# Attention, a triangle update and two norms: three engine queues in another order

## The chip, the core and the metric

The kernel runs on one core of a Trainium2 chip. The core has five engines that work through queues of their own, each strictly in program order: TensorE (PE, matrix products), VectorE (DVE), ScalarE (ACT, activations), GpSimd (POOL) and SyncE (SP, which issues the DMAs). They wait for each other on semaphores. A wait holds up all that is queued behind it on its engine. The metric is the time of one execution on the device in microseconds (us), and lower is better.

## The reference, cut to what matters

The input is 32 images of 16 x 16 pixels with 32 channels, in float32. Eight layers follow each other, each as `x = x + layer(norm(x))`. Only the parts that the change touches are shown.

```python
# layer 0: linear attention, 4 heads of 32
q = softmax(q, over channels) / sqrt(32);  k = softmax(k, over pixels);  v = v / 256
out = einsum(einsum(k, v), q) @ w_out + b_out;  out = norm(out) * ln_scale
# layer 1: spectral convolution over the 256 pixels, with filters made of phi, sigma, M_u, M_phi
# layer 2: "triangle"
a = sigmoid((x @ Wa1 + ba1) * (x @ Wa2 + ba2));  b = sigmoid((x @ Wb1 + bb1) * (x @ Wb2 + bb2))
g = sigmoid(x @ Wg + bg);  z = einsum('bikc,bkjc->bijc', a, b);  y = g * (norm(z) @ Wz + bz)
# layer 3: recurrent cell;  layer 4: scan over rows;  layer 5: mixture of experts
# layer 6: scan over rows;  layer 7: recurrent cell
norm(v) = (v - mean(v, over channels)) / sqrt(var(v, over channels) + eps)
```

## The kernel before, in words

**Layout.** The 128 partitions hold 4 groups of 32 channels (NQ = 4), and each group holds 8 images (G = 8) of 256 pixels. `xQ` is the running sum, of 2,048 columns, in four chunks (CH = 4) of 512 columns. In one cut a chunk is a pair of images, in another it is a quarter of the pixels of all images. `bank` is the accumulator memory of TensorE, eight banks of 512 columns.

**A norm** runs chunk by chunk through three engines. PE multiplies by a centring matrix (`ln_centre`, line 207), ACT squares (`ln_square`, L266), PE spreads the mean of the squares (`ln_spread`, L213), ACT takes Ln and Exp (`ln_rstd`, L272 and L277), and DVE multiplies (L259, L1303 and others). Two norms, number 2 (ahead of the spectral convolution) and number 7 (ahead of the second scan), read `xQ` in pairs of images and write it in quarters of the pixels. For quarters 0 and 1 they centre straight from `xQ`: `ln_centre_r` (L229) makes four products per quarter, each of 32 output rows and 512 columns that step by four elements through all images, so all of `xQ` must be there. For quarters 2 and 3, DVE first copies strips (`copy_strips`, L254), and PE centres the strips. DVE starts these copies when all of `xQ` is there. The order on PE is centre 0, centre 1, spread 0, centre 2, spread 1, centre 3, spread 2, spread 3.

**Attention** (PE L575 to L663, ACT L985 to L1045, DVE L1213 to L1265) works through 16 units u: K product, Q product, V product, transposition of exp(K), context product. Each engine has its loop over i, and lags the units:
- PE in step i: K(i), filters, Q(i), V(i), transpose(i-1) (L605), context(i-2) (L617), in every fourth step an output product, filters.
- ACT in step i: in steps 2 and 3 first two scalings of the spectral weights (L1028), then eviction of filters (`a_filters`, L1019), `a_k(i)` (Exp, L990), `a_kn(i-1)` (L1011), `a_v(i)` (L999), `a_q(i)` (Exp of Q, L1005); in step 0 then `filter_setup` (L961 to L967), which prepares the spectral weights; filters.
- DVE in step i: `v_k(i)` (maximum, L1216), `v_qw(i-1)` (L1234 to L1239, which needs `a_q(i-1)`), `v_q(i)` (L1223 to L1229), then the context scaling of unit i-2. In step 1 it also computes the fraction weights (L1201 to L1210), which ACT's scalings wait for.
- POOL: `q_normalise(u)` (L471), and behind units 1, 2 and 3 a sum of spectral weights (L487). The last of these sums releases the filters.

The 16 filters of the spectral convolution (`filters`, PE) stand two to a step, in steps 5 to 12. The second of a pair overwrites the accumulator of the first, so it waits for ACT's eviction, and the first of the next step waits likewise. After the sixteenth, SP issues 16 DMAs (L445) that spread the filters.

**Triangle.** Once the spectral convolution ends (L707), PE transposes the last quarter (16 small products), DVE adds it, and norm 3 of the last quarter follows (`normalise(3)`, L1303). Then PE makes the 16 `a` products, the 16 `b` products (128 x 128 each) and the gate. DVE adds a bias in halves (L1333) and multiplies (L1338) to get `a_in`, then `b_in`. ACT takes the sigmoid of `a` (L1069) and of `b` (L1073), and then copies three of eight masked blocks of `a` (`a_bd`, L1078, ACT_BD = 3), and DVE the other five (L1343). The 128 products of a with b (L745) wait for all of them.

**Experts.** Eight products (g = 0 to 7) end the layer; each pair fills one accumulator bank, and DVE adds it to `xQ` (L1539). Norm 7 comes next.

`keep_busy` (L532) issues products whose results nobody reads, between waits. A helper records `full` at L532 too, so many kinds of product show that line.

## Time and profile before

| | us |
|---|---|
| median of 3 executions (lowest, highest) | 474.16 (472.72, 477.4) |
| the profiled execution: its own time | 474.01 |
| its span in the trace | 471.9 |

Busy shares of the span: PE 90%, weight loads of PE 55%, DVE 52%, ACT 38%, POOL 7%. The profile has 2.11 us outside the span. Where stages lie in the trace, in us from the start of the span:

| stage | from | to |
|---|---|---|
| attention units, without filters | 17 | 47 |
| attention units with filters, and the last three | 47 | 112 |
| norm 1 and the sum; norm 2 | 112 | 136 |
| spectral convolution | 136 | 247 |
| triangle up to the products of a with b | 247 | 271 |
| rest of the triangle, recurrent cell, norm 5, scan, experts | 271 | 397 |
| norm 7 | 397 | 409 |
| second scan, recurrent cell, store | 409 | 472 |

A matmul in float32 shows as two records (x2), so that 8 products are x16.

### The profile page before, as it was taken

The numbers are of one execution on the slowest core, as the hardware profiler recorded it, in microseconds if no ns is written. First come the engines' busy times: TensorE is split into PE (matmuls) and PEld (weight loads), VectorE is DVE, ScalarE is ACT, GpSimd is POOL, SyncE is SP. The second block draws the span as 40 slices with busy tenths as digits, with TensorE's granted clock in tenths as the row PEclk, the third lists the DMA queues.
The fourth block names the chain that finished last, engine by engine and source line by source line (L and its number), as shares of the span: only waits on it lengthen the run. The fifth ranks groups of instructions, "written<-read, shape, count | busy, mean of one in ns | idle before, by whom it ended". The sixth has DMA issues, their size and how long they took to land.

```text
span 471.9 us, 7130 instructions
## 1 busy us (share of the span) xinstructions
PE 424.3 (90%) x2880; PEld 260.1 (55%) x2880; DVE 246.3 (52%) x486; ACT 181.3 (38%) x373; POOL 32.9 (7%) x39
## 2 busy tenths in 40 slices
PE   6967999999879999998999999897999899999990
PEld 2434656554255567653765555394475474475590
DVE  3499677786778050106103746646534628434735
ACT  1776777755530002001102643454504631414360
POOL 0037222222000000000000000000000000000000
PEclk8898999999999999999999999998999999999997
DMA  9940000079940000000002000000000000000003
GB/s 222 135 97 1 1 1 1 2 160 219 203 90 0 1 0 0 1 0 0 1 0 47 0 1 3 0 1 2 0 1 2 2 0 1 0 1 1 0 1 90
DMA packets 6479, 15.24 MB, mean 32 GB/s; under 512 B 2718, under 2 KB 5422, under 8 KB 5806
## 3 DMA queue, kind: packets, MB, share of 16 engines
q1 hardware_dynamic: 5870, 14.25, 14.9%
q8 instruction: 23, 0.38, 0.3%
q10 hardware_dynamic: 576, 0.52, 0.3%
q14 instruction: 10, 0.08, 0.1%
HBM read 5.86 MB, written 1.05 MB: 15 GB/s over the span
## 4 chain that ended last, share of the span: by engine, by line
PE 66%; DVE 17%; ACT 10%; issue 3%; DMA 1%; POOL 1%; POOLq 0%; SPq 0%; DVEq 0%; ACTq 0%
PE bank L673 20%; PE bank L532 17%; PE bank L213 6%; PE bank L861 5%; PE bank L207 4%; PE bank L806 4%; PE bank L817 3%; PE bank L229 2%; ACT lnv L272 2%; ACT rs L277 2%; DVE xn L259 1%; DVE xQ L1294 1%; DMA xR<-in_x 1%; PE bank L605 1%; ACT arena L1019 1%
## 5 line engine op out<-in xcount | busy, mean ns | idle before, releaser
L673 PE MATMUL bank<-xn,arena 128*128 128x512 f32 (+15 forms) x332 | 88.9, 427 | 2.4 <-DVE xn L259 2.4
L673 PEld LDWEIGHTS bank<-xn,arena 128*128 128x128 f32 x332 | 56.3, 190 | 36.0 <-issue 27.0
L266 ACT ACTIVATE sq<-bank 128x512 f32<-128x512 f32 x36 | 21.3, 591 | 118.0 <-PE bank L207 98.3
L532 PE MATMUL bank<-sb_consts 128*128 128x512 f32 (+1 forms) x116 | 52.9, 569 | 1.6 <-ACT arena L1153 1.6
L532 PE MATMUL bank<-xn,sb_w_attn 128*128 128x512 f32 x64 | 35.4, 644 | 4.8 <-ACT attn_scratch L990 3.7
L213 PE MATMUL bank<-sq,sb_consts 128*128 128x512 f32 x72 | 38.7, 623 | 0.7
L272 ACT ACTIVATE lnv<-bank 128x512 f32<-128x512 f32 x36 | 21.5, 597 | 35.4 <-PE bank L213 35.3
L1303 DVE TENSOR_TENSOR arena<-bank,rs 128x512 f32<-128x512 f32 x4 | 4.2, 1038 | 51.4 <-ACT rs L277 51.4
L532 PEld LDWEIGHTS bank<-sb_consts 128*128 128x128 f32 x116 | 20.5, 194 | 18.7 <-issue 16.5
L861 PEld LDWEIGHTS bank<-arena,sb_w_late 128*128 128x128 f32 x180 | 23.0, 191 | 11.1 <-DVE arena L1470 8.0
L861 PE MATMUL bank<-arena,sb_w_late 128*128 128x128 f32 x180 | 27.2, 287 | 1.7 <-DVE arena L1470 1.3
L806 PE MATMUL bank<-arena,sb_consts 128*128 128x128 f32 x144 | 27.7, 276 | 0.7 <-DVE arena L1420 0.7
L207 PE MATMUL bank<-xQ,sb_consts 128*128 128x512 f32 x40 | 23.0, 664 | 5.6 <-DVE xQ L1183 3.1
L817 PE MATMUL bank<-arena,sb_w_late 128*128 128x128 f32 x144 | 27.9, 276 | 0.0
L1294 DVE TENSOR_TENSOR xQ<-bank,xQ 32x128 f32<-32x128 f32 x48 | 18.3, 382 | 13.7 <-PE bank L673 13.1
L1107 ACT ACTIVATE arena<-bank 128x128 f32<-128x128 f32 x72 | 19.9, 277 | 14.3 <-PE bank L817 14.2
L213 PEld LDWEIGHTS bank<-sq,sb_consts 128*128 128x128 f32 x72 | 12.6, 193 | 21.8 <-issue 13.5
L471 POOL TENSOR_TENSOR attn_scratch<-attn_scratch 128x512 f32<-128x512 f32 x16 | 20.3, 1272 | 58.1 <-DVE attn_scratch L1239 57.9
L277 ACT ACTIVATE rs<-lnv 128x512 f32<-128x512 f32 x36 | 22.7, 629 | 1.1
L806 PEld LDWEIGHTS bank<-arena,sb_consts 128*128 128x128 f32 x144 | 21.7, 192 | 2.3 <-issue 2.3
L1470 DVE SCALAR_TENSOR_TENSOR arena<-bank,xn 128x128 f32<-128x128 f32 x30 | 8.7, 291 | 26.7 <-PE bank L861 25.9
L532 PEld LDWEIGHTS bank<-wvo,xn 128*128 128x128 f32 x128 | 17.7, 200 | 8.1 <-issue 8.1
(193 smaller groups left out, 623.5 us busy)
## 6 DMA issues: line engine op xcount, KB each, us to landing
arena<-arena SPq DMA_DIRECT2D x4, 1024.0 KB, 16.0
arena<-arena SPq DMA_DIRECT2D x4, 512.0 KB, 8.7
arena<-in_w_spec SPq DMA_DIRECT2D x2, 720.0 KB
sb_w_late<-in_w_late SPq DMA_DIRECT2D x1, 1100.5 KB, 22.8
xR<-in_x SPq DMA_DIRECT2D x4, 256.0 KB, 4.5
arena<-arena SPq DMA_DIRECT2D x4, 256.0 KB, 4.1
sb_w_attn<-in_w_attn SPq DMA_DIRECT2D x1, 641.0 KB, 7.4
arena<-in_w_spec SPq DMA_DIRECT2D x2, 256.0 KB
```

What stands on the lines that cost most here:

```text
L207: pe.matmul(bank[:, centre_bank(i), :], centre, src, start=True, stop=True).then_inc(S("ln_centred"), 1)
L213: pe.matmul(bank[:, var_bank(i), :], mean32, sq[:, i % 2, :], start=True, stop=True)\
L266: act.activation(sq[:, i % 2, :], bank[:, centre_bank(i), :], ACT.Square).then_inc(S("ln_squared"), 1)
L272: act.activation(lnv[:, i % 2, :], bank[:, var_bank(i), :], ACT.Ln, bias=LN_EPS[i // CH])\
L277: act.activation(rs[:, i % 2, :], lnv[:, i % 2, :], ACT.Exp, scale=-0.5).then_inc(S("ln_rstd"), 1)
L471: link(pool.tensor_tensor(qn[:, u % QN, :], qe[:, u % 2, :], qn[:, u % QN, :], ALU.mult))
L532: return mm(ps, lhsT, rhs, start=True, stop=True)
L673: return mm(bank[:, k, lo * B:hi * B], lhs, cols[:, at * B:(at + hi - lo) * B], start=start, stop=stop, **kw)
L806: mm(place(s, h), ident, z_[:, h, s % RES, :, :], start=True, stop=False)
L817: mm(place(s_, h), rvt[i], before(h, s_ % RES), start=False, stop=True)\
L861: last = mm(bank[:, 4 + h % 2, 0:P], band[i][:, w, :], carry[:, h - 1, w:w + 4, :], start=(w == 0), stop=(w == 2))
L1294: last = dve.tensor_tensor(xs, stu[C * r:C * r + C, :, G * q:G * q + G].rearrange("p t g -> p g t"), xs, ALU.add)
```

## The change

- Attention. PE: the step becomes K(i), transpose(i-1), Q(i), filters, V(i), context(i-2), ... . ACT: the step becomes (scalings in steps 2 and 3), `a_q(i-1)`, `a_kn(i-1)`, `a_k(i)`, filters, (in step 0 the rest of norm 0), `a_v(i)`, (in step 0 `filter_setup`), filters.
- Norms 2 and 7. PE centres quarters 0 and 1 in pieces: for each pair of images as soon as it is there, 8 products of 128 columns. In norm 2 this starts after the second pair. In norm 7 two of the four pieces stand within the experts' last products. The order behind is spread 0, centre 2, spread 1, centre 3, spread 2, spread 3.
- Triangle. The `a` products of the first three quarters stand in places of `keep_busy`, ahead of the last quarter's norm; DVE adds the first half of the bias ahead of `normalise(3)`. ACT copies two of its blocks of `a_bd` ahead of the sigmoid of `b`, and one behind. Products of `keep_busy` change from (3, 4) to (2, 2), and three single ones go.

```diff
-BUSY_ATTN, BUSY_TRI, BUSY_SCAN, BUSY_LOGITS = 4, (3, 4, 6, 1), 3, 2
+BUSY_ATTN, BUSY_TRI, BUSY_SCAN, BUSY_LOGITS = 4, (2, 2, 6, 1), 3, 2
-ACT_BD = 3
+ACT_BD, ACT_BD_FIRST = 3, 2
...
+        def centre_images(pe, k, j):
+            for q in range(STRIP_Q):
+                for r in range(NQ):
+                    last = pe.matmul(bank[C * r:C * r + C, q, 2 * TC * j:2 * TC * j + 2 * TC],
+                                     centre[:, C * q:C * q + C], xQ[:, 2 * j:2 * j + 2, r:T:NQ], start=True, stop=True)
+                if j == CH - 1:
+                    last.then_inc(S("ln_centred"), 1)
+
+        def ln_pe_images(pe, k):
+            def centre_strip(q):
+                pe.wait_ge(S("strips"), NQ_STRIPS * R_NORMS.index(k) + q - STRIP_Q + 1)
+                ln_centre(pe, CH * k + q, strips[:, q - STRIP_Q, :])
+            ln_spread(pe, CH * k)
+            centre_strip(2)
+            ln_spread(pe, CH * k + 1)
+            centre_strip(3)
+            ln_spread(pe, CH * k + 2)
+            ln_spread(pe, CH * k + 3)
...
# PE, attention
-                for m in filter_turn(u, 0):
-                    filters(m)
+            def attn_q_v(u):
+                j, q = divmod(u, NQ)
                 if u >= 1:
                     pe.wait_ge(S("q_shift"), u)
                 full(bank[:, 2, :], wq[:, q, :], flat(xn, j)).then_inc(S("q_ps"), 1)
+                for m in filter_turn(u, 0):
+                    filters(m)
...
                     attn_mid(i - 1)
+                if i < U:
+                    attn_q_v(i)
...
# PE, norm 2
-            ln_pe_r(pe, 2, xQ, lambda: pe.wait_ge(S("x_attn"), CH))
+            for j in range(CH):
+                pe.wait_ge(S("x_attn"), max(2, j + 1))
+                centre_images(pe, 2, j)
+            ln_pe_images(pe, 2)
...
# PE, triangle
-            keep_busy(BUSY_STU, 6)
+            def a_columns(ms):
+                for m in ms:
+                    pe.wait_ge(S("ln_applied"), 3 * CH + m // 4 + 1)
+                    last = full(bank[:, m // 4, (m % 4) * P:(m % 4 + 1) * P],
+                                xnH[:, m, :, :].rearrange("p g w -> p (g w)"), wa)
+                    if m % 8 == 7:
+                        last.then_inc(S("ab_ps"), 1)
+            pe.wait_ge(S("w_late_in"), 16)
+            a_columns(range(0, 4))
             pe.wait_ge(S("stu_rows"), 1)
...
-            keep_busy(BUSY_STU, 6)
+            a_columns(range(4, 8))
             pe.wait_ge(S("x_stu"), CH)
             ln_centre(pe, CH * LN_TRI + CH - 1, tokens(xQ, CH - 1))
-            keep_busy(1, 6)
+            a_columns(range(8, 12))
             ln_spread(pe, CH * LN_TRI + CH - 1)
             keep_busy(BUSY_TRI[0], 6)
             pe.wait_ge(S("ln_applied"), 4 * CH)
+            a_columns(range(12, 16))
...
# PE, norm 7, and within the experts' last products
-                    ln_pe_r(pe, k, xQ, lambda: pe.wait_ge(S("x_moe"), CH))
+                    for j in (2, 3):
+                        pe.wait_ge(S("x_moe"), j + 1)
+                        centre_images(pe, k, j)
+                    ln_pe_images(pe, k)
...
+                    if g in (5, 7):
+                        pe.wait_ge(S("x_moe"), g // 2 - 1)
+                        centre_images(pe, 7, g // 2 - 2)
...
# ACT, attention
+                if 0 <= i - 1 < U:
+                    a_q(i - 1)
+                    a_kn(i - 1)
+                if i < U:
+                    a_k(i)
                 for m in filter_turn(i, 0):
                     a_filters(m)
-                if i < U:
-                    a_k(i)
...
-                    a_q(i)
...
# ACT, triangle
+            act.wait_ge(S("a_s"), 1)
+            blocks_of_a(range(ACT_BD_FIRST))
             act.wait_ge(S("b_in"), 1)
...
+            blocks_of_a(range(ACT_BD_FIRST, ACT_BD)).then_inc(S("a_bd"), 1)
...
# DVE, triangle
+            link(add_ab_bias(0, 0))
             normalise(3)
...
+                    link(add_ab_bias(1, 0))
+                last = add_ab_bias(k, 1)
```

## Rows read from the trace of the kernel before

**Rows 1.** The page's chain of work that ended last, shares of the span by engine
```profile
PE 66%; DVE 17%; ACT 10%; issue 3%; DMA 1%; POOL 1%; POOLq 0%; SPq 0%; DVEq 0%; ACTq 0%
```

**Rows 2.** Timeline, PE in filter units: start, length, instruction, [idle before <- releaser]
```profile
51.40 1.12 PE L532 MATMUL bank<-xn,sb_w_attn 128*128 128x512 f32 x2
...
69.58 1.12 PE L532 MATMUL bank<-xn,sb_w_attn 128*128 128x512 f32 x2
...
71.12 0.82 PE L532 MATMUL bank<-sb_w_stu,arena 64*128 64x256 f32 x4 [0.42 <-ACT arena L1019]
...
75.39 1.13 PE L532 MATMUL bank<-xn,sb_w_attn 128*128 128x512 f32 x2
```

**Rows 3.** Timeline, ACT in the same unit
```profile
71.99 1.05 ACT L1019 ACTIVATE arena<-bank 128x512 f32<-128x512 f32 x1 [0.92 <-PE bank L532]
```

**Rows 4.** Timeline, ACT at the start of attention
```profile
25.05 0.84 ACT L967 ACTIVATE odd_sig<-sig 32x1 f32<-32x1 f32 x4
...
28.62 0.63 ACT L1005 ACTIVATE attn_scratch<-attn_scratch 128x512 f32<-128x512 f32 x1 [0.71 <-DVE attn_scratch L1229]
30.78 2.19 ACT L1028 ACTIVATE arena<-arena,fw 128x1024 f32<-128x1024 f32 x2 [1.52 <-DVE fw L1210]
```

**Rows 5.** Timeline, DVE at the start of attention, first of `v_qw(0)`, of `v_qw(1)`, and `v_k(4)`
```profile
24.79 0.70 DVE L1234 TRANSPOSE_TENSOR_REDUCE attn_scratch<-attn_scratch 128x16 f32<-128x512 f32 x1
...
31.20 0.70 DVE L1234 TRANSPOSE_TENSOR_REDUCE attn_scratch<-attn_scratch 128x16 f32<-128x512 f32 x1
...
40.66 0.69 DVE L1216 TENSOR_REDUCE attn_scratch<-bank 128x2 f32<-128x512 f32 x1 [0.67 <-PE bank L532]
```

**Rows 6.** Timeline, POOL and PE up to the first filter
```profile
43.15 1.27 POOL L471 TENSOR_TENSOR attn_scratch<-attn_scratch 128x512 f32<-128x512 f32 x1 [1.60 <-DVE attn_scratch L1239]
...
47.13 0.82 PE L532 MATMUL bank<-sb_w_stu,arena 64*128 64x256 f32 x4 [2.88 <-POOLq L489]
```

**Rows 7.** Timeline of PE, and a window of 2 us (PEclk after POOL's column)
```profile
34.01 2.76 PE L532 MATMUL bank<-xn,sb_w_attn 128*128 128x512 f32 x4 [2.53 <-ACT attn_scratch L990]
...
36.00:38.00 2.00, 2.00 (x8) 1.48 (x8) 1.93 (x4) 2.00 (x3) 1.09 (x2) 0.50 0.01 4
```

**Rows 8.** Timeline, PE and DVE in norm 2
```profile
120.59 1.88 PE L532 MATMUL bank<-sb_consts 128*128 128x512 f32 x4
...
123.73 4.96 DVE L254 COPY attn_scratch<-xQ 32x512 f32<-32x512 f32 x8
...
123.75 3.79 PE L229 MATMUL bank<-xQ,sb_consts 128*32 128x512 f32 x16 [1.29 <-DVE xQ L1273]
...
127.47 1.12 PE L213 MATMUL bank<-sq,sb_consts 128*128 128x512 f32 x2
...
134.60 1.02 DVE L259 TENSOR_TENSOR xn<-bank,rs 128x512 f32<-128x512 f32 x1 [0.20 <-ACT rs L277]
```

**Rows 9.** Timeline, PE at the end of the experts and in norm 7
```profile
392.07 3.62 PE L532 MATMUL bank<-arena 128*128 128x256 f32 x16
396.47 3.79 PE L229 MATMUL bank<-xQ,sb_consts 128*32 128x512 f32 x16 [0.78 <-DVE xQ L1539]
```

**Rows 10.** Timeline, PE, DVE and ACT in the triangle
```profile
248.15 1.08 PE L532 MATMUL bank<-arena,sb_consts 128*32 128x128 f32 x32
...
256.01 3.81 PE L532 MATMUL bank<-sb_w_late,xR 128*128 128x128 f32 x32 [0.45 <-DVE xR L1303]
...
261.12 1.23 DVE L1338 TENSOR_TENSOR arena<-arena 128x1024 f32<-128x1024 f32 x1
262.38 2.03 ACT L1069 ACTIVATE arena<-arena 128x1024 f32<-128x1024 f32 x1 [6.80 <-DVE arena L1338]
...
266.03 2.13 ACT L1073 ACTIVATE arena<-arena 128x512 f32<-128x512 f32 x2 [1.62 <-DVE arena L1338]
...
268.07 3.21 ACT L1078 ACTIVATE arena<-arena,sb_consts 128x1024 f32<-128x1024 f32 x3
...
271.33 1.94 PE L745 MATMUL bank<-arena 128*32 128x128 f32 x61 [1.07 <-ACT arena L1078]
```

More of the change, by code:

```diff
@@ L716, in _ @@
             last.then_inc(S("stu_cols"), 1)
-            keep_busy(BUSY_STU, 6)
+            a_columns(range(4, 8))
             pe.wait_ge(S("x_stu"), CH)
             ln_centre(pe, CH * LN_TRI + CH - 1, tokens(xQ, CH - 1))
-            keep_busy(1, 6)
+            a_columns(range(8, 12))
             ln_spread(pe, CH * LN_TRI + CH - 1)
             keep_busy(BUSY_TRI[0], 6)
-            pe.wait_ge(S("w_late_in"), 16)
             pe.wait_ge(S("ln_applied"), 4 * CH)
-            for k in range(2):
-                for m in range(16):
-                    cols = (xnH[:, m, :, :].rearrange("p g w -> p (g w)") if k == 0
-                            else xm[:, m * P:(m + 1) * P])
-                    last = full(bank[:, 4 * k + m // 4, (m % 4) * P:(m % 4 + 1) * P], cols, [wa, wb][k])
-                    if m % 8 == 7:
-                        last.then_inc(S("ab_ps"), 1)
+            a_columns(range(12, 16))
+            for m in range(16):
+                last = full(bank[:, 4 + m // 4, (m % 4) * P:(m % 4 + 1) * P], xm[:, m * P:(m + 1) * P], wb)
+                if m % 8 == 7:
+                    last.then_inc(S("ab_ps"), 1)
             pe.wait_ge(S("a_pre"), 1)
@@ L1029, in _ @@
                             .then_inc(S("wm_scaled"), 1)
+                if 0 <= i - 1 < U:
[3 more added lines that the diff above has]
+                    a_k(i)
                 for m in filter_turn(i, 0):
                     a_filters(m)
-                if i < U:
-                    a_k(i)
                 if i == 0:
                     ln_rstd(act, 3)
-                if 0 <= i - 1 < U:
-                    a_kn(i - 1)
                 if i < U:
                     a_v(i)
-                    a_q(i)
                 if i == 0:
@@ L1069, in _, with blocks_of_a @@
             act.activation(a_s[:, :], a_in[:, :].rearrange("p (h m) -> p m h", h=16), ACT.Sigmoid).then_inc(S("a_s"), 1)
+            def blocks_of_a(gs):
+                for g in gs:
+                    ins = act.activation(a_bd[:, :, g, :], a_s.rearrange("p (m i) -> p m i", i=16), ACT.Copy,
+                                         scale=par16[:, g:g + 1])
+                return ins
+            act.wait_ge(S("a_s"), 1)
+            blocks_of_a(range(ACT_BD_FIRST))
             act.wait_ge(S("b_in"), 1)
@@ L1075, in _ @@
             last.then_inc(S("b_s"), 1)
-            act.wait_ge(S("a_s"), 1)
-            for g in range(ACT_BD):
-                last = act.activation(a_bd[:, :, g, :], a_s.rearrange("p (m i) -> p m i", i=16), ACT.Copy,
-                                      scale=par16[:, g:g + 1])
-            last.then_inc(S("a_bd"), 1)
+            blocks_of_a(range(ACT_BD_FIRST, ACT_BD)).then_inc(S("a_bd"), 1)
             act.wait_ge(S("gate_ps"), 1)
@@ L1323, in _, with add_ab_bias @@
             dve.tensor_tensor(x3, bank[:, 3, :].rearrange("p (r n g) -> p g n r", r=NQ, g=G), x3, ALU.add).then_inc(S("x_stu"), 1)
+            pre4 = ab_pre.rearrange("p (m n) -> p m n", n=2 * CT)
+            def add_ab_bias(k, half):
+                dve.wait_ge(S("ab_ps"), 2 * k + half + 1)
+                first = 4 * k + 2 * half
+                return dve.tensor_tensor(pre4[:, 32 * half:32 * half + 32, :],
+                                         bank[:, first:first + 2, :].rearrange("p k (m n) -> p (k m) n", n=2 * CT),
+                                         ab_bias[:, k:k + 1, :].to_broadcast([P, 32, 2 * CT]), ALU.add)
+            dve.wait_ge(S("w_late_in"), 16)
+            link(add_ab_bias(0, 0))
             normalise(3)
-            dve.wait_ge(S("w_late_in"), 16)
             for k in range(2):
@@ L1328, in _ @@
                     dve.wait_ge(S("a_in"), 1)
-                pre4 = ab_pre.rearrange("p (m n) -> p m n", n=2 * CT)
-                for half in range(2):
-                    dve.wait_ge(S("ab_ps"), 2 * k + half + 1)
-                    first = 4 * k + 2 * half
-                    last = dve.tensor_tensor(pre4[:, 32 * half:32 * half + 32, :],
-                                             bank[:, first:first + 2, :].rearrange("p k (m n) -> p (k m) n", n=2 * CT),
-                                             ab_bias[:, k:k + 1, :].to_broadcast([P, 32, 2 * CT]), ALU.add)
+                    link(add_ab_bias(1, 0))
+                last = add_ab_bias(k, 1)
                 last.then_inc(S(["a_pre", "b_pre"][k]), 1)
```

## The prediction

> **What bounds the kernel now.** I read the page first: the chain that ended last runs two thirds on PE, the rest mostly on DVE and ACT [rows 1]. No engine bounds the whole, so I read the timeline of each changed stage, one engine at a time. The reader should see there who is waited for last.
>
> Filter units of attention. PE works without a gap from the first filter of a unit to the next K product: 71.12 to 75.39, 4.27 us. One stall stands ahead: K starts at 69.58 and would hand over after 0.86 (its 1.12 less a tail of 0.26), at 70.44, but the filter waits for ACT's eviction until 71.12 [rows 2]. So a unit of 5.81 is 5.13 of PE's work and 0.68 of stall. ACT idles at least 0.92 of it [rows 3], so it carries 4.9 or less.
>
> Start of attention. PE waits for others: the first filter for POOL at 47.13 [rows 6], K(3) for ACT at 34.01 [rows 7]. The real chain there runs between DVE and ACT.
>
> Norm 2. PE's eight strided products fill 123.75 to 127.47, and only then comes the first spread; the last multiplication starts 7.13 later, at 134.60 [rows 8]. Triangle: from the first `a` product at 256.01 a chain PE, DVE, ACT leads to 271.33 [rows 10]. The spectral convolution in between is PE's and is not touched; SP's filter DMAs precede it, move with the last filter and are needed in the same order, so I cost them at nothing.
>
> **Attention, the start.** In step 0 `a_q(0)` now stands behind `filter_setup`, which ends at 25.05 + 0.84 = 25.89 [rows 4]. It takes 0.63, so `v_qw(0)` starts near 26.6 instead of 24.79 [rows 5]: DVE is 1.8 late, and with it the fraction weights. ACT's two scalings then run at 32.6 to 34.7 instead of 30.78 [rows 4], and `a_q(1)`, formerly at 28.62, is queued behind them: `v_qw(1)` starts near 35.4 instead of 31.20, 4.2 late [rows 5]. From there DVE runs unbroken and swallows its one wait, 0.67 ahead of `v_k(4)` [rows 5]. So `v_qw(3)`, POOL's normalisation at 43.15, its sum and the first filter come 3.5 late: 50.6 instead of 47.13 [rows 6]. The scalings of step 3 delay `a_q(2)` too, but DVE is not ready for it earlier. Behind `a_k(2)`, also late, K(3) on PE starts near 36.9; PE idles about 4.2 ahead of it instead of 2.5.
>
> At the first filter PE has already done the transposition (0.53 in the order of a unit) and Q (0.96), which formerly followed. Of the 4.27 up to the next K [rows 2], 2.8 remain: K(6) starts at 53.4 instead of 51.40. Net 2.0 late.
>
> **Attention, the filter units.** The first filter now has the transposition and Q ahead of it, 1.4 us of work, against the 0.68 that ACT was late. The second filter follows V and context, and needs the first's eviction: filter at 2.3 of the cycle, ACT 0.87 later, 1.05 long, ends at 4.2; PE arrives at 4.3. That is tight, and `a_kn` and `a_k` now stand ahead of the eviction on ACT; they wait for `v_k`, which ends at 1.8, so `a_k` ends at 3.0, in time for 3.1. Hence 5.13 to 5.2 per unit. Seven units follow K(6); in two of them the output product ahead already hid half of the stall. Saved: 5 x 0.68 + 2 x 0.34 = 4.1, less 0.2 for the tight wait, 3.9. The last three units, without filters, are paced by DVE's 4.8 per unit; I take 0.2 there. Sum of attention: 2.0 - 3.9 - 0.2 = **-2.1**. Ends: 0, if units save only half; -4, if the late start costs nothing beyond 1.8.
>
> **Norm 2.** No row shows the small strided products. Their bounds: a quarter of the eight old ones, 3.53 without the tail, 0.88 per piece [rows 8]; or half of 32 records of 128 columns without stride, 0.5 [rows 10]; with their 64 records against 16, 1.1 is the upper end. The old ones have the same stride, so I take 0.9. PE is in `keep_busy` until 122.3 [rows 8]. The pieces end at 123.2, 124.1, 125.0 and 125.9, all behind the sums, so the last sum (123.7) no longer sets them. The first spread starts near 126.4, when the square of quarter 0 is there, instead of 127.47. Behind it, DVE's strips end at 128.7 as before [rows 8], and the third and fourth centring, the squares and rstd keep their 7.1. **-1.05.** With 0.5 per piece the second strip becomes the bound, and the gain is 1.6; with 1.1 it is 0.3. The Trainium skill (SBUF — State Buffer, Door 1) says that reads pay a penalty at each new line of 16 bytes, and the step here is 16 bytes; by it 0.9 holds, by the unstrided row the sum would be 0.9 lower over both norms.
>
> **Norm 7.** PE makes a product in 0.43 (3.62 for eight) [rows 9]. The first piece stands behind g = 5 and delays g = 6 and 7 by 0.9, and so the last sum, DVE's copies of strips and all behind them; the second piece, behind g = 7, delays nothing of DVE. The chain on PE: 392.07 + 6 x 0.43 = 394.65; piece 395.55; two products 396.4; pieces to 397.3, 398.2, 399.1. The square and the first spread follow at 399.6, against 396.47 + 3.72 = 400.19. Strips, 0.9 late, end at 402.35, 2.8 behind the first spread (as before, 2.3 behind a spread 0.6 later is 402.5 for the centring that needs them), so they bind by nothing. **-0.5**, between 0 and -0.9. A changed tiling of the array (32 output rows to 128 and back) occurs twice more here. The row shows little: 32 records fill 1.08 where four abreast need 0.85 [rows 10]. The Trainium skill (TensorEngine Tiling (Array Packing), Key Properties) says that a change of mode drains the engine; by 0.2 for each pair the gain here would be 0.1.
>
> **Triangle.** `normalise(3)` stays where it was: the early `a` products take 0.91 each four (3.65 for sixteen), the place of a `keep_busy` product (0.86), and the first half of the bias on DVE fits into its wait for ACT's rstd. After 256.05: four `a` products 1.22 to their end, one bias half 1.26, `a_in` 1.26, sigmoid of `a` 2.06, two blocks 2.08, sigmoid of `b` 2.04, one block 1.1 [rows 10]: 267.1 instead of 271.33. The side paths: `b_in`, by two bias halves and a product from 259.8, is there at 263.6, ahead of ACT's 264.0; DVE's five blocks of 0.68 then end at 267.0, and the gate on PE at 264.1. **-4.2**; 4.4 at best, 3.2 if a wait of 1 us not shown appears on DVE. ACT's next, the sigmoid of the gate, moves along. Two `keep_busy` products fewer leave PE idle for about 1.4 twice.
>
> **Sum.** -2.1 - 1.05 - 0.5 - 4.2 = -7.8. The profiled execution took 474.01, 0.15 under the median of the runs shown: **466.2**. Ends: 0 - 0.3 - 0 - 3.2 = -3.5, 470.5; -4 - 1.6 - 0.9 - 4.4 = -10.9, 463.1. A measurement of this kernel tells about 1% (4.7 us) from no change.
>
> **Rivals.**
> 1. ACT becomes the bound of the filter units: the eviction, now behind `a_k`, comes late each time, and no unit gains. For: the margin is 0.1. Against: its load is 4.9 of 5.13. Attention +1.8 instead of -2.1: 470.1, within 1%.
> 2. PE's clock falls and stays: the change lengthens PE's wait ahead of K(3) to 4.2. After the old wait of 2.5 the window from 36 shows a granted clock of 0.50, 1.2 GHz, and two products take 2.76 [rows 7], where two of the same width take 1.88 at full clock [rows 8]. If the shorter bursts of units 3 to 5 keep it there into the filter units, each costs up to 4.1 more (5.13 at near half speed). Two such units eat the whole gain; from the third the kernel is slower, and with four it is 474.0 - 7.8 + 16.4 = 482.6. Against: before, it recovered by the next unit, and stayed up through the wait ahead of 47.13.
> 3. The late start is absorbed (the order on ACT harmless): the first filter at 47.1 with the transposition and Q done. Attention -5.6: 462.7. Against: a queue in order leaves no way round.
> 4. The norms give nothing, because pieces queue behind `keep_busy` and the strips bind: 467.8.
>
> **Chances.** Forecast (463.9 to 468.5) 0.62; rival 1 0.15; rival 2 0.04; rival 3 0.07; rival 4 0.12. The range 463.0 to 470.5 leaves out rival 2, most of rival 3 and a part of rival 1. Faster by over 1% (under 469.3): forecast, 3, 4, and a fifth of rival 1: 0.84. Within: 0.12. Slower: 0.04.
>
> **What would show it.** In the timeline after: `a_q(0)` at 25.9, `a_q(1)` behind the scalings at 34.7, first filter at 50.6, filter units of 5.2, no wait of the first filter for ACT; the last sum of attention 2.1 earlier; pieces of 0.9; first spread of norm 2 1.0 ahead of its old place behind the sum; L745 4.2 closer to the end of L707. I am wrong if the filter units stay near 5.8, if the granted clock stays at 0.5 past 50, or if another releaser than ACT stands ahead of L745.

## The result, and the profile after

The changed kernel takes **469.39 us** (median of 20 runs, lowest 466.08), the kernel before 473.70 beside it (20 runs, lowest 472.65). The ratio of the times is **0.9883, 95% interval 0.9860 to 0.9906**: 5.5 us faster, where 7.8 were forecast. The ratio leaves out after's four slowest runs (474.9 to 476.3, at a mean granted clock of 0.951 to 0.957); with them the medians are 4.3 apart. The profiled execution of after took 466.08 us itself, 3.3 less than its median: it is the fastest of its runs, and its pair with the profiled execution of before (474.01) overstates the gain. Where the difference between the two traces comes from is worked out stage by stage below.

The page of after, its first lines, the clock's line of the slices and the shares of the chain (against rows 1):

```profile
span 464.3 us, 7301 instructions
...
PEclk9998999999989999999999999999999999999997
...
PE 69%; DVE 15%; ACT 9%; issue 4%; DMA 1%; POOL 1%; POOLq 0%; SPq 0%; DVEq 0%; ACTq 0%
```

DVE's and ACT's shares of the chain fell by three points together, PE's rose by three. The digits 8 of the clock's line hold short stretches of lower clock.

To see where the time went I measured seven stages in every trace, each from the start of one instruction to the start of another, so that what one stage loses isn't counted in the next: start (to the first K product), attention (to norm 2's strip copy), norm 2 (to the first product of the spatial unit), spatial unit (to the `both` transposition, L707 before), triangle (to L745 before), then the middle part up to the first of the experts' last products, and the rest. In us, worked out from the timelines:

```
kernel                    start  attention norm 2  spatial triangle  middle  rest    span
before                    17.42   106.31   11.94   110.59   25.07   120.74  79.80  471.87
after                     14.38   105.01   10.98   113.82   20.87   119.33  79.89  464.28
attention_alone           16.13   105.00   11.94   113.94   25.22   120.88  79.79  472.90
triangle_alone            16.22   107.81   11.94   112.24   20.86   120.85  79.78  469.70
norm2_alone               17.34   106.31   10.98   113.82   25.22   120.88  79.82  474.37
norm7_alone               16.23   107.99   11.94   110.57   25.22   120.75  79.74  472.44
after_stu_filled          17.52   104.99   10.97   110.61   20.85   120.66  79.74  465.34
after_all_filled          14.65   104.98   10.99   110.62   20.88   120.75  79.75  462.62
before_all_filled         14.36   107.73   11.94   110.59   25.06   120.84  79.78  470.30
after_early_q             16.09   102.21   10.96   110.58   20.87   120.89  79.75  461.35
filled_early_q            14.50   101.68   10.97   110.61   20.87   122.16  79.76  460.55
filled_early_q_no_norm7   14.49   101.80   10.96   110.61   20.88   120.97  79.85  459.56
filled_early_q_order      14.66   107.75   10.97   110.59   20.89   120.97  79.78  465.61
filled_old_attention      14.59   107.19   10.98   110.61   20.87   122.67  79.77  466.68
```

Read by column. Where the clock is full a stage repeats to hundredths, in kernels that differ elsewhere: norm 2 is 11.94 or 10.98, the triangle 25.1 or 20.87. Attention gives 1.3, norm 2 0.96, the triangle 4.2, the rest with norm 7 nothing: 6.5. But three stages that the change doesn't touch differ too: in after the spatial unit is 3.2 longer, the start 3.0 and the middle 1.4 shorter. That is how 6.5 become the 7.6 between the two spans.

**The attention.** PE in one filter unit of after, against rows 2 (start, length, instruction):

```profile
67.31 1.12 PE L554 MATMUL bank<-xn,sb_w_attn 128*128 128x512 f32 x2
68.28 0.60 PE L630 MATMUL bank<-sb_consts,attn_scratch 128*128 128x128 f32 x4
68.71 1.02 PE L554 MATMUL bank<-xn,sb_w_attn 128*128 128x512 f32 x2
69.67 0.81 PE L554 MATMUL bank<-sb_w_stu,arena 64*128 64x256 f32 x4
70.41 1.16 PE L554 MATMUL bank<-wvo,xn 128*128 128x128 f32 x8
71.50 0.46 PE L642 MATMUL bank<-attn_scratch 128*32 128x32 f32 x32
71.89 0.82 PE L554 MATMUL bank<-sb_w_stu,arena 64*128 64x256 f32 x4
72.64 1.12 PE L554 MATMUL bank<-xn,sb_w_attn 128*128 128x512 f32 x2
```

No wait is left, but K to K is 5.33, not 5.13. ACT at the start, and PE up to K(6), against rows 4, 6 and 7:

```profile
22.88 0.63 ACT L1047 ACTIVATE attn_scratch<-attn_scratch 128x512 f32<-128x512 f32 x1
...
29.55 2.19 ACT L1070 ACTIVATE arena<-arena,fw 128x1024 f32<-128x1024 f32 x2 [4.15 <-DVE fw L1256]
31.64 0.61 ACT L1047 ACTIVATE attn_scratch<-attn_scratch 128x512 f32<-128x512 f32 x1
```

```profile
33.78 1.31 PE L554 MATMUL bank<-xn,sb_w_attn 128*128 128x512 f32 x2 [3.98 <-ACT attn_scratch L1032]
...
47.47 0.82 PE L554 MATMUL bank<-sb_w_stu,arena 64*128 64x256 f32 x4 [0.90 <-POOLq L511]
...
50.44 1.12 PE L554 MATMUL bank<-xn,sb_w_attn 128*128 128x512 f32 x2
```

Counted from the first K product (14.38 here, 17.42 before), the first filter comes at 33.1 instead of 29.7 and K(6) at 36.1 instead of 34.0: 3.4 and 2.1 late.

**Norm 2 and norm 7**, PE and DVE, against rows 8 and 9:

```profile
118.05 3.87 PE L253 MATMUL bank<-xQ,sb_consts 128*32 128x128 f32 x64
122.17 1.12 PE L213 MATMUL bank<-sq,sb_consts 128*128 128x512 f32 x2 [0.25 <-ACT sq L288]
...
119.39 5.05 DVE L276 COPY attn_scratch<-xQ 32x512 f32<-32x512 f32 x8
...
129.30 1.01 DVE L281 TENSOR_TENSOR xn<-bank,rs 128x512 f32<-128x512 f32 x1 [0.20 <-ACT rs L299]
```

```profile
384.39 2.86 PE L554 MATMUL bank<-arena 128*128 128x256 f32 x12
387.18 1.10 PE L253 MATMUL bank<-xQ,sb_consts 128*32 128x128 f32 x16
388.21 1.13 PE L554 MATMUL bank<-arena 128*128 128x256 f32 x4
389.27 2.92 PE L253 MATMUL bank<-xQ,sb_consts 128*32 128x128 f32 x48
392.45 1.13 PE L213 MATMUL bank<-sq,sb_consts 128*128 128x512 f32 x2 [0.26 <-ACT sq L288]
...
395.21 1.12 PE L207 MATMUL bank<-attn_scratch,sb_consts 128*128 128x512 f32 x2
...
389.37 0.69 DVE L1590 TENSOR_TENSOR xQ<-xQ,bank 128x512 f32<-128x512 f32 x1 [1.40 <-PE bank L554]
390.10 5.06 DVE L276 COPY attn_scratch<-xQ 32x512 f32<-32x512 f32 x8
```

Norm 2's last multiplication starts 9.91 behind the strip copies, before 10.87 [rows 8]. Norm 7's first spread starts 8.06 behind the first of the experts' last products, before 400.19 - 392.07 = 8.12 [rows 9], and the fourth centring starts as DVE's copies end, at 395.2.

**The triangle**, ACT and PE, against rows 10:

```profile
257.72 2.01 ACT L1111 ACTIVATE arena<-arena 128x1024 f32<-128x1024 f32 x1 [4.17 <-DVE arena L1389]
259.76 2.19 ACT L1114 ACTIVATE arena<-arena,sb_consts 128x1024 f32<-128x1024 f32 x2
261.86 2.10 ACT L1123 ACTIVATE arena<-arena 128x512 f32<-128x512 f32 x2
263.86 1.14 ACT L1114 ACTIVATE arena<-arena,sb_consts 128x1024 f32<-128x1024 f32 x1
```

```profile
265.06 3.20 PE L781 MATMUL bank<-arena 128*32 128x128 f32 x107 [1.16 <-ACT arena L1114]
```

ACT runs without a gap, and its last block releases PE, as the forecast's chain had it.

**TensorE's clock.** Windows at the start of the spatial unit, first after, then before (window, length, busy PE, PEld, DVE, ACT, POOL, granted clock, DMA share, GB/s):

```profile
130.00:132.00 2.00, 1.63 (x4) 1.41 (x5) 0.37 (x2) 0.00 (x0) 0.00 (x0) 0.53 0.00 0
132.00:134.00 2.00, 2.00 (x11) 1.96 (x11) 2.00 (x2) 0.00 (x0) 0.00 (x0) 0.62 0.00 0
```

```profile
136.00:138.00 2.00, 2.00 (x17) 1.97 (x15) 1.07 (x2) 0.00 (x0) 0.00 (x0) 1.00 0.00 0
```

PE's first product of the unit and the wait ahead of it, after and then before:

```profile
130.37 4.96 PE L703 MATMUL bank<-xn,arena 128*128 128x256 f32 x20 [2.40 <-DVE xn L281]
```

```profile
135.67 6.64 PE L673 MATMUL bank<-xn,arena 128*128 128x256 f32 x35 [2.40 <-DVE xn L259]
```

The wait is 2.40 in both. Behind it after runs at the lower level (1.2 GHz) for most of two windows, and is at 1.00 from 134 on; before stays at 1.00. The two windows are short of full clock by 2 x 0.47 + 2 x 0.38 = 1.7 us. A second such stretch follows a wait of 2.28 inside the unit, at 218 to 224 (0.71, 0.50, 0.93: again 1.7). Together 3.4, against 3.2 that the unit is longer. I call such a stretch a dip.

Dips explain the start and the middle as well. Three windows of before, one at the start and two at the end of the experts, and a product between the last two:

```profile
10.00:12.00 2.00, 2.00 (x4) 0.93 (x3) 1.64 (x4) 0.60 (x1) 0.00 (x0) 0.50 0.93 123
386.00:388.00 2.00, 1.30 (x29) 1.27 (x28) 0.00 (x0) 1.88 (x2) 0.00 (x0) 0.76 0.00 0
388.00:390.00 2.00, 2.00 (x11) 1.17 (x10) 1.44 (x4) 0.00 (x0) 0.00 (x0) 0.50 0.00 0
```

```profile
386.73 1.73 PE L532 MATMUL bank<-arena 128*32 128x32 f32 x32 [0.70 <-ACT arena L1163]
```

Over the fourteen kernels of the table, the start is 14.4 to 14.7 with no dip in it (after and the six with a filled start, below), 16.1 to 16.2 with one, 17.3 to 17.5 with two on end (before has them at 8 to 16). The middle is 119.33 without a dip in the experts, in after alone; 120.7 to 121.0 with one; 122.2 and 122.7 with two. So the profiled execution of after was spared three dips that cost before time, and had two in the spatial unit that before didn't have. A dip doesn't always cost time: between 26 and 40, in the attention, 0.5 at most, and at norm 5 (324 to 330 in before) nothing that the middle shows.

### The profile page after: what moved, and what is told of

Same layout as the page of the kernel before. It is cut to its first block, busy times and chain, and to the rows that moved or that the text cites. A ratio compares the mean times of both kernels' runs of the same rounds, so it can differ in the third digit from the quotient of the medians.

```text
span 464.3 us, 7301 instructions
## 1 busy us (share of the span) xinstructions
PE 419.3 (90%) x2964; PEld 261.2 (56%) x2964; DVE 246.3 (53%) x486; ACT 182.2 (39%) x373; POOL 33.0 (7%) x39
## 3 DMA queue, kind: packets, MB, share of 16 engines
HBM read 5.86 MB, written 1.05 MB: 15 GB/s over the span
## 4 chain that ended last, share of the span: by engine, by line
PE 69%; DVE 15%; ACT 9%; issue 4%; DMA 1%; POOL 1%; POOLq 0%; SPq 0%; DVEq 0%; ACTq 0%
PE bank L703 21%; PE bank L554 18%; PE bank L213 6%; PE bank L900 5%; PE bank L207 4%; PE bank L842 4%; PE bank L853 3%; ACT lnv L294 2%; PE bank L253 1%; ACT rs L299 1%; DVE xQ L1340 1%; DMA xR<-in_x 1%; DVE xn L281 1%; PE bank L642 1%; ACT sq L288 1%
## 5 line engine op out<-in xcount | busy, mean ns | idle before, releaser
L703 PE MATMUL bank<-xn,arena 128*128 128x512 f32 (+15 forms) x332 | 92.2, 438 | 2.4 <-DVE xn L281 2.4
L703 PEld LDWEIGHTS bank<-xn,arena 128*128 128x128 f32 x332 | 58.2, 196 | 37.3 <-issue 28.2
L554 PE MATMUL bank<-sb_consts 128*128 128x512 f32 (+1 forms) x104 | 46.2, 555 | 1.6 <-ACT arena L1199 1.6
L900 PEld LDWEIGHTS bank<-arena,sb_w_late 128*128 128x128 f32 x180 | 23.0, 191 | 11.2 <-DVE arena L1521 8.0
L554 PEld LDWEIGHTS bank<-sb_consts 128*128 128x128 f32 x104 | 17.9, 190 | 15.5 <-issue 13.4
L207 PE MATMUL bank<-xQ,sb_consts 128*128 128x512 f32 x40 | 20.8, 606 | 4.5 <-DVE xQ L1340 2.3
L853 PEld LDWEIGHTS bank<-arena,sb_w_late 128*128 128x128 f32 x144 | 21.9, 192 | 0.2
```

The lines of the kernel that those rows point to most:

```text
L207: pe.matmul(bank[:, centre_bank(i), :], centre, src, start=True, stop=True).then_inc(S("ln_centred"), 1)
L554: return mm(ps, lhsT, rhs, start=True, stop=True)
L703: return mm(bank[:, k, lo * B:hi * B], lhs, cols[:, at * B:(at + hi - lo) * B], start=start, stop=stop, **kw)
L853: mm(place(s_, h), rvt[i], before(h, s_ % RES), start=False, stop=True)\
L900: last = mm(bank[:, 4 + h % 2, 0:P], band[i][:, w, :], carry[:, h - 1, w:w + 4, :], start=(w == 0), stop=(w == 2))
```

## The experiments

**Each part by itself.** Four kernels, each the kernel before with one part: the orders of the attention, the triangle's, norm 2's centring, norm 7's.

> The kernel before with the attention change alone. Theory of the trace after (a filter unit costs PE 5.33 us instead of the 5.13 forecast, first filter 3.4 us late as forecast): -1.3 us, ratio 0.997; filter units 5.3 us, PE without a wait in them. Forecast: -2.1, ratio 0.9956. Rival, the late start costs more than the units give: ratio over 1.

Measured: 475.82 us, ratio 1.0012 (0.9976 to 1.0049). The attention is 105.00, shorter by 1.3, and the spatial unit 113.94, longer by 3.35: the gain doesn't show in the time. The rival had a ratio over 1, and the interval holds 1; but its way is out, since the attention is shorter.

> The kernel before with the triangle change alone. Forecast and trace after both say -4.2 us (from the last product of the spectral convolution to the products of a with b 20.9 us instead of 25.1), ratio 0.991. Rival, fewer products of keep_busy cost part of it by the clock: granted clock below 1 in that stretch, ratio 0.994 or more.

Measured: 471.40 us, ratio 0.9941 (0.9907 to 0.9975). The triangle stage is 4.2 shorter, as in after. In time 2.8 of it arrive; the profiled execution has a dip at 136 to 140, in the spatial unit (112.24), and one at 46 to 52, in the attention (107.81 instead of 106.31). In the triangle stage itself the clock stays at 1.00, so the rival's fewer products of `keep_busy` aren't what took the rest.

> The kernel before with the new centring of norm 2 alone. Trace after: -0.96 us from the last sum of attention to the first product of the spectral convolution (11.0 instead of 12.0), ratio 0.998. Rival: the clock falls at the start of the spectral convolution more often than before, which takes 1.5 us each time: ratio 1.000 to 1.001, and a window at 0.5 to 0.6 there.

Measured: 475.39 us, ratio 1.0032 (1.0011 to 1.0053), slower, though norm 2 itself is 0.96 shorter. Its trace, in windows:

```profile
134.00:136.00 2.00, 1.37 (x3) 1.17 (x4) 0.57 (x1) 0.00 (x0) 0.00 (x0) 0.59 0.00 0
136.00:138.00 2.00, 2.00 (x10) 1.95 (x8) 1.53 (x2) 0.00 (x0) 0.00 (x0) 0.56 0.00 0
...
224.00:226.00 2.00, 2.00 (x3) 0.67 (x2) 0.00 (x0) 0.00 (x0) 0.00 (x0) 0.50 0.00 0
```

The same two dips as in after, again 113.82 for the unit, as the rival had it, but twice. An edit that saves 1 us ahead of the wait is followed by 3.2 lost behind it; why just here isn't shown.

> The kernel before with the new centring of norm 7 alone (two pieces within the experts' last products). Trace after: 0, since DVE's strips end 1.4 us later and set the fourth centring (16.7 us from the first of the last products to the second scan, as before), ratio 1.000. Forecast: -0.5, ratio 0.999.

Measured: 474.87 us, ratio 1.0010 (0.9984 to 1.0036). Norm 7's stage is as long as before. The four ratios together make 0.9995, nearly nothing, and the whole change makes -1.2%: the parts aren't additive in time, though they are in the stages.

**Taking the waits away.** If the dips of the spatial unit come from PE's waits, throw-away products in the waits must remove them. After the last spread of norm 2, and ahead of the third centring in the spatial unit:

```diff
             ln_pe_images(pe, 2)
+            pe.wait_ge(S("ln_logged"), CH * 2 + 1)
+            keep_busy(2, 4)
             pe.wait_ge(S("ln_applied"), 3 * CH)
...
                         if k == bk and m == m_centre:
+                            if j == 2:
+                                keep_busy(2, 3)
                             pe.wait_ge(S("x_stu"), j + 1)
```

> The kernel after, with four more of its own throw-away 128x512 products on TensorE: two between norm 2's last spread product and the wait for its normalised pixels ahead of the spatial unit (idle 2.40 us in the trace after), two ahead of the wait for the update that the third centring inside the spatial unit needs (idle 2.28). Each product takes 0.86 us of otherwise idle time, so 1.7 fits into either wait. Theory A (what the trace after lost against the forecast is the granted clock: stretches of some 3.4 us at 0.50 that begin where TensorE has just waited for 2 us or more, and each costs 1.5 to 1.7 us): the stretches at 130 to 134 and 218 to 224 are gone, the spatial unit's 184 products take 47.97 instead of 49.51 us, the whole unit 110.6 instead of 113.8, and the time falls by 1.5 to 3.2 us against the kernel after. Rival B (the stretches of low clock come from the load of the centring products by pairs of images, or by chance, and not from the waits): they stay, at the same or another place, and the time is that of the kernel after, 469.4, within 0.7.

Measured: 467.07 us, ratio 0.9822 (0.9775 to 0.9868). The unit takes 110.61, and a window and the first product are these:

```profile
134.00:136.00 2.00, 2.00 (x16) 1.98 (x15) 0.29 (x1) 0.00 (x0) 0.00 (x0) 1.00 0.00 0
...
133.48 4.73 PE L705 MATMUL bank<-xn,arena 128*128 128x256 f32 x26 [0.68 <-DVE xn L281]
```

Theory A holds at both places. The median fell by 2.3 from that of after, in another set of runs, and the intervals of the two ratios overlap by a little (0.9860 and 0.9868), so it is the stage that shows the effect. The profiled execution has dips at 8 to 16 and 28 to 34, where after's has one, at 34 to 38.

```diff
-BUSY = {2: 2, 3: 6, 4: 1, 5: 1, 7: 0}
-BUSY_ROW, BUSY_START, BUSY_BACK = 1, 3, 1
+BUSY = {2: 2, 3: 6, 4: 1, 5: 2, 7: 0}
+BUSY_ROW, BUSY_START, BUSY_BACK = 1, 5, 1
...
                 pe.wait_ge(S("ln_applied"), j + 1)
+                if u == 3:
+                    keep_busy(3, 4)
```

> The kernel before last with the same kind of products in three more waits: two at the start (idle 1.99 us before the first centring product), three ahead of the attention's fourth K product (idle 3.98 in the trace after), one ahead of norm 5 (idle 1.24). Theory A: the stretch of clock 0.50 at 34 to 38 goes too, where TensorE bounds the stage only in part, so 0.5 to 1.5 us more than with the four products alone: 465 to 467 us. Rival B: as the kernel after, 469.4. Rival C: the waits were short of what the added products need (a product is issued as a whole and can delay the one that follows by up to 0.9), so the added ones cost 0.5 to 1 us more than they bring.

The edit shown is what it adds to `after_stu_filled`. Measured: 464.41 us, ratio 0.9772 (0.9724 to 0.9820), 2.7 less again, more than expected. All of it is the start, 14.65 instead of 17.52. No stage is longer: rival C falls. But the other half of the expectation missed. The attention is 104.98, as before, and has two dips on end at 26 to 34, behind a wait of 2.60 ahead of K(2) that I hadn't filled. And the product at norm 5 takes away a dip there in this trace without shortening the middle (120.75 against 120.66). Counted in the kernel, the added products are ten, not the nine of the next expectation: two, three and one here, four before.

> The kernel before with the same nine throw-away products in the same five waits. If theory A holds, both kernels now run without most of the stretches of low clock, and their difference is what the change itself moves: 1.3 in the attention, 1.0 in norm 2, 4.2 in the triangle, none in norm 7, 6.5 us in all, a ratio of 0.986. The kernel before itself gains little in the spatial unit, where its profiled run had no such stretch, and some 1 to 2 us at the start: 471 to 473. Rival B: 473.7 as before, and the difference to the filled kernel after stays at what chance makes of it.

Measured: 472.35 us, ratio 0.9940 (0.9902 to 0.9978). On the same chip the two filled kernels are 464.41 and 472.35: **7.9 us apart, 0.983**. Their spans differ by 7.7: triangle 4.2, norm 2 0.95, attention 2.75. Of the last, some 1.4 is a dip at 44 to 50 that the profile of before doesn't have (its attention is 106.31, against 107.73 here). Ahead of it the old order waits for POOL before its first filter:

```profile
42.00:44.00 2.00, 0.16 (x2) 0.19 (x2) 1.93 (x5) 0.44 (x1) 1.64 (x1) 1.00 0.00 0
46.00:48.00 2.00, 2.00 (x9) 1.70 (x8) 1.42 (x2) 0.52 (x3) 0.00 (x0) 0.50 0.00 0
```

So the new order also shortens a wait that can cost clock, 2.88 before [rows 6], 0.90 after. Without that dip the two would be 6.3 us apart.

**The late start.**

```diff
                 if i in (2, 3):
+                    a_q(i - 1)
...
                 if 0 <= i - 1 < U:
-                    a_q(i - 1)
+                    if i > 3:
+                        a_q(i - 1)
                     a_kn(i - 1)
...
                 if i == 0:
+                    a_q(0)
                     filter_setup()
```

> The kernel after, where ScalarE takes the exponential of q of unit 0 ahead of the filters' setup, and those of units 1 and 2 ahead of the scalings of the filters' weights, as the kernel before had them; all else of the new order stays. Theory (the late exponentials of q at the start shift the first filter by 3.4 us and the seventh K product by 2.1): both come back, the attention takes 2 to 3.4 us less, 101.6 to 103 instead of 105.0, and the time is 466 to 467.4. Rival D (the first filter waits for GpSimd's masks and the scaled weights, whatever the exponentials of q do, and the later scalings shift it as much): the attention is shorter by under 0.7 and the time within 1 us of the kernel after.

Measured: 464.09 us, ratio 0.9774 (0.9722 to 0.9825). The attention is 102.21, 2.8 less than in after. ACT and PE:

```profile
27.30 0.63 ACT L1047 ACTIVATE attn_scratch<-attn_scratch 128x512 f32<-128x512 f32 x1 [0.58 <-DVE attn_scratch L1279]
29.45 2.19 ACT L1072 ACTIVATE arena<-arena,fw 128x1024 f32<-128x1024 f32 x2 [1.52 <-DVE fw L1260]
```

```profile
46.39 0.81 PE L554 MATMUL bank<-sb_w_stu,arena 64*128 64x256 f32 x4 [0.90 <-POOLq L511]
```

The exponential of unit 1 is ahead of the scalings again, and the first filter comes 30.3 behind the first K product (16.09), not 33.1. The late start was a real cost of the change. The total fell by more than 2.8, since this execution has no dip in the spatial unit (110.58); that part isn't the edit's by anything shown.

**Both together, and norm 7 and the order taken up again.** `filled_early_q` has both edits, and `keep_busy(u, 4)` ahead of K(2) too.

> The kernel after with both: the early exponentials of q of after_early_q and the throw-away products of after_all_filled, and two more of these ahead of the third K product (TensorE idle 2.21 us there). If the two effects are separate, the attention takes about 102.2 us as in after_early_q, the spatial unit 110.6, the start (up to the first K product) 14.4 to 14.7, and the time is 464.4 less 2.8, that is 461 to 462.5. Rival: the added products ahead of the third and fourth K product now delay them, since the waits are shorter by 0.4 to 0.9 with the early exponentials: attention 103 to 104, time 463 to 464.5.

Measured: **461.11 us**, ratio 0.9721 (0.9681 to 0.9761): the fastest, 2.8% under before, 1.6 points better than the change itself. Its runs lie between 460.61 and 463.13. Attention 101.68, so the added products delay nothing.

> As filled_early_q, but norm 7 again as in the kernel before: all 64 centring products by strips after the last update of the experts. Theory (norm 7's edit gives nothing, since the third and fourth strip copies, 5.06 us on VectorE, end as late as before, and the last spread waits for them): the same time within 0.3 us, and the same 16.3 to 16.4 us from the first of the experts' last products to the copy of the scan's carry. Rival: the pieces between the experts' last products, slower with their stride of a row (1.03 against about 0.95 us of 16), cost what they save at the end: up to 0.5 faster without the edit. Second rival, the forecast's term: 0.5 slower without it.

Measured: 461.38 us, ratio 0.9723 (0.9685 to 0.9761). From the first of the experts' last products to the carry's copy it takes 16.40, with the edit 16.32. Norm 7's edit is worth nothing that can be measured.

```diff
                 full(bank[:, 2, :], wq[:, q, :], flat(xn, j)).then_inc(S("q_ps"), 1)
-                for m in filter_turn(u, 0):
-                    filters(m)
...
+                for m in filter_turn(i, 0):
+                    filters(m)
                 if i < U:
                     attn_q_v(i)
+                late_ctx = bool(filter_turn(i, 1))
-                if 0 <= i - 2 < U:
+                if not late_ctx and 0 <= i - 2 < U:
                     attn_ctx(i - 2)
...
                 for m in filter_turn(i, 1):
                     filters(m)
+                if late_ctx:
+                    attn_ctx(i - 2)
```

> As filled_early_q, but in each unit of the attention with filters TensorE's order is K, transposes, filter, Q, V, filter, context instead of K, transposes, Q, filter, V, context, filter. In the trace after, a unit with filters takes 5.33 us, where 5.13 were forecast, and the V products take 1.09 from start to start ahead of the context products, but 0.89 ahead of the transposes in the trace before. Theory (the narrow 128x32 products of the context wait for the deep pipeline of the four V products, a cost of this hand-over alone): with a filter between them the V step falls to about 0.9, the unit to about 5.13 to 5.2, the attention by 7 times 0.15 to 0.2, or 1.0 to 1.4 us. Rival (the context products cost the same hand-over behind any other product, then the filter's step is longer by 0.2): the unit stays at 5.33. Second rival: the second filter, now 0.4 us earlier behind the first, waits for ScalarE's eviction of it (1.05 us), and the unit gets longer, 5.4 to 5.6.

Measured: 467.40 us, ratio 0.9831 (0.9793 to 0.9869): slower than `filled_early_q` by 1.1 points of the ratio, some 5 us. One unit on PE:

```profile
68.90 0.60 PE L630 MATMUL bank<-sb_consts,attn_scratch 128*128 128x128 f32 x4
69.75 0.82 PE L554 MATMUL bank<-sb_w_stu,arena 64*128 64x256 f32 x4 [0.25 <-ACT arena L1070]
70.50 1.12 PE L554 MATMUL bank<-xn,sb_w_attn 128*128 128x512 f32 x2
71.46 1.05 PE L554 MATMUL bank<-wvo,xn 128*128 128x128 f32 x8
72.52 0.82 PE L554 MATMUL bank<-sb_w_stu,arena 64*128 64x256 f32 x4
73.27 0.46 PE L642 MATMUL bank<-attn_scratch 128*32 128x32 f32 x32
```

My theory falls: behind a filter instead of the context the V step is 1.06, hardly less than 1.09, so the cost isn't that of the context alone. And the wait for ACT is back (0.25, the transposition's step 0.85 instead of 0.43), since ACT's eviction of the second filter now comes late. This unit is 5.72, nearly the old 5.81. The place that the change gave the first filter, behind Q, is what hides the eviction. The very first filter now waits 2.45 for POOL, with Q behind it instead of ahead, and a dip follows at 44 to 50: K(6) comes 2.0 later, counted from the first K product. The seven units behind it take 42.84 instead of 39.07, 3.8 more, since in two of them the second filter waits for ACT as well (0.53 and 0.55). Together 5.8 of the attention's 6.1.

> As filled_early_q (461.1 us), but the attention in the order of the kernel before on both TensorE and ScalarE; norm 2, norm 7, the triangle and the throw-away products stay. The exponentials of q come as early as in filled_early_q, the first filter starts as early, and the stretches of low clock at the start are filled in both, so the difference is what the new order of the units with filters and of the last units is worth by itself. Theory (seven units at 5.81 instead of 5.33 us, 3.4 in all, and the last three units 0.2 to 0.9 shorter): the attention takes 105.5 to 106.2 us instead of 101.7, and the time is 464.8 to 465.8. Rival (the late exponentials were part of what the new order needs, so the early ones would have cost it something that the old order does not pay): a difference under 3 us, attention under 104.7, time under 464.2.

Measured: 468.24 us, ratio 0.9853 (0.9800 to 0.9906), 7.1 above `filled_early_q`; by the ratios, each against the kernel before beside it, 6.3, and by the spans 6.2. The attention is 107.19 against 101.68. The rival falls; the theory's size was short by 1 to 1.7 us, which is a dip at 44 to 50 behind the wait of 2.81 for the first filter, that I had not filled. Less this, the new order is worth about 4 in the attention once its start isn't late: the seven units behind K(6) take 42.19 in the old order and 39.07 in the new.

## Why the prediction was right or wrong

**The sign, the range and the triangle were right.** The median of 469.39 lies in the stated range, 463.0 to 470.5, though above the forecast's own band, 463.9 to 468.5; by the ratio, 0.9883, it would be 468.2 and inside. The triangle was forecast at -4.2 and is -4.20; the chain a-half, `a_in`, sigmoid, two blocks, `b_s`, one block [rows 10] came out link by link, with ACT as releaser. Norm 2 was forecast at -1.05 and is -0.96: the pieces take 0.97 each (3.87 for four), not 0.9. The unstrided bound of 0.5 is out. The Trainium skill (SBUF — State Buffer, Door 1) charges reads that step by 16 bytes, and the trace agrees as far as it goes: 0.97, where 0.5 was worked out from products without a stride.

**Attention: -1.3 instead of -2.1.** The start went as forecast, link by link: scalings, then `a_q(1)` behind them, first filter 3.4 late (3.5), K(6) 2.1 late (2.0). So did the disappearance of the stall. The term "5.13 of PE's work and 0.68 of stall" was mis-sized. I had cut a K product to 0.86, but its step to the transposition is 0.97, and V's is 1.09 instead of 0.89, against 0.43 instead of 0.53 for the transposition: +0.11 + 0.20 - 0.10 = 0.21. The unit saves 0.48, not 0.68. Over the seven units behind K(6) that is 3.1 (from 42.17 to 39.06) where 3.9 were forecast, and this 0.8 is all that the attention fell short. I had taken the durations of PE's steps as the product's own, but each belongs to a pair of neighbours, and the new order makes other pairs. About 0.1 goes with each neighbour: V between Q and the context takes 0.98 in after; with the transpositions behind it instead 0.89, with a filter ahead of it instead 1.09. The Trainium skill (TensorEngine Tiling (Array Packing), Key Properties) says that PE drains when the tiling changes. It bears on V into context (128 rows, then 32 columns) and on filters of 64 rows, and the steps agree with it; no run takes the drain apart from other causes.

**Norm 7: 0 instead of -0.5.** The half of rival 4 that put the bound on the strips holds. The piece between the experts' products took 1.03 and the products on either side 0.2 more each than forecast (2.79 for six, 1.06 for two, against 2.6 and 0.86), so the first spread gained 0.06 of 0.6, and the strips behind the later last sum took the rest. The other half of the rival, that norm 2's pieces queue behind `keep_busy` and gain nothing, fell.

**The step that failed** is one that I wrote in half a sentence: the spatial unit "is PE's and is not touched", and has no term in the sum. It isn't touched, but 2.40 and 2.28 us waits of PE stand ahead of it and in it, and behind them the clock may drop. In seven profiled kernels with those waits the unit took 110.6 three times, 112.2 once, 113.8 or 113.9 three times; in seven with products in them it took 110.6 every time. This is shown. With the waits filled on both sides the change is worth 7.9 us, the forecast 7.8; that agreement is luck, since 1.4 of it is the attention's dip in the old order, which fills the place of the mis-sized unit and of norm 7. What the change itself moves is 6.5 in the stages.

**Rival 2** named the clock, and at the place that it named it cost little: after waits 3.98 ahead of K(3), and runs at half clock behind it, but from 38 on its windows are at 1.00 again. It named a fall that stays, and looked only at the attention. What it should have priced is a fall of one stretch at up to 1.7 us each, in every stage that PE bounds: the start, the spatial unit, the experts. **Rival 1** fell (no unit waits for ACT), though the order experiment shows how near it was. **Rival 3** fell for the change as it stands.

**Open.** Which waits bring a dip in a given kernel isn't settled: before and norm2_alone have the same 2.40 and differ. Nor is a wait of 2 us needed: thirteen of the fourteen profiles have a dip at the end of the experts, where PE's last waits in before are 1.60, 0.31 and 0.70 with short products between. These were not filled. After's runs spread from 466.08 at a mean clock of 0.982 to 470.27 at 0.965, so in sum the dips differ between runs of one kernel. The Trainium skill (TensorE: Matmul & The Clock Gate, Part 1) says that the number of products which run at the lower level at a kernel's start varies from run to run; the starts here differ too, between kernels that are equal up to there, but nothing here shows that a kernel's own dips are chance alone. Each stage length is that of one execution.

## What to carry to other kernels

When a stage that PE bounds begins behind a wait of PE (2.3 to 2.4 us here), price one dip of the clock (1.4 to 1.7 us here) into the range of every change, even one that lies elsewhere, and compare stages, not totals, before you credit an edit of under 1%. Ten throw-away products in five waits brought 5.0 us on after and 1.9 on before; in the traces only those at the start and in the spatial unit shortened a stage. When PE's order is changed, take each step's length from start to start with its neighbour, and treat new neighbours as unknown by 0.1 to 0.2 us each. When an engine's queue is reordered for the steady state, look at the first rounds by themselves: keeping the old order there brought 2.8 us.

## What the runs showed of the hardware

Waits of 2.3 to 2.4 us on PE were enough for the granted clock to be at 0.5 in the following windows, in some kernels and not in others. Four products of 0.86 us put into two of them removed 3.2 us (113.82 to 110.61). At the end of the experts the clock fell to 0.50 behind waits of 1.6 at most in thirteen of fourteen profiles. A dip cost 1.4 to 1.7 us where PE bounds, and nothing that shows at norm 5. The step of the four V products (128x128, f32) took 0.89 between Q and the transpositions, 0.98 between Q and a context, 1.06 between Q and a filter of 64 rows, and 1.09 between a filter and the context of 128x32.
